# Four of the last sequence's eight attention steps placed ahead of the experts, in a kernel that runs two layers as one program

## The chip, the core and the metric

The kernel runs on one core of a Trainium2 chip. A core has TensorE (PE, matrix products, with PEld for its weight loads), VectorE (DVE), ScalarE (ACT), GpSimd (POOL) and SyncE (SP, which here only issues DMAs). Each engine works through its own list of instructions in order; semaphores hold an engine until another has got far enough. The metric is the device time of one execution in microseconds (us), as the median of several runs.

## The reference, cut to what matters

```python
x = L0_attn_x                                   # 8 sequences, 512 rows, 128 columns
xn = layernorm(x)
s = attention(xn, Wq, Wk, Wv, Wo)               # two query heads, one key/value head, rope, causal softmax
g = silu(experts(xn))                           # router, top 2 of 8 experts, F = 512, gelu
x = x + s * g
xn = layernorm(x)
s = mixer(xn)                                   # rmsnorm, 7-tap convolution, gated scan over the rows, gated ffn
g = silu(tanh(xn @ W @ A1 @ A2 + b))
x = x + s * g
```

Attention and experts of layer 0 read the same `xn` and don't need each other. The product `s * g` needs both.

## The kernel before

**The order of the stages.** There is no scheduler: each engine's list is written out by hand. (1) Layer norm, router and projections. (2) Attention of sequences 0 to 6 (`NB` = 7 is the number of the last one). Beside it POOL scatters the 2 x 4096 chosen rows to a DRAM buffer `slots_x`, sorted by expert, with 64 indirect DMAs in bursts of four. (3) The experts: 71 tiles of 128 rows (`SLOT_TILES`); PE does for each tile the gate product (L928), the up product (L937) and the down product (L946), one tile behind. (4) Attention of the last sequence. (5) Layer 1, sequence by sequence. Its first sequence has a long start: DVE adds the two expert rows of each token (`d_first_both`, L1463), multiplies with the attention (`d_first_product`, L1467), applies the gate (`d_first_gate`, L1472), adds to x (L1502), takes statistics (L1509), POOL takes the roots, DVE scales (L1480), and PE turns the result (`d_turn_scaled`, L983).

**One attention step.** A sequence has eight steps k, in the order of `STEPS = [(3, 0), (0, 0), (3, 1), (0, 1), (2, 0), (1, 0), (2, 1), (1, 1)]`: (tile of 128 rows, head). Tile i looks at i+1 tiles of keys, so the steps 0 to 3 and the steps 4 to 7 have the same sum of columns (1280 each). A step goes through four engines: scores on PE (L804, L806), row maximum on DVE (L1329), exponent on ACT (L1799), transposes on PE (L822), copy to SBUF on ACT (L1808), product with the values on PE (`weigh`, L844); for head 0 a scaled copy on ACT (`head0`, L1817), for head 1 a sum on DVE (`combine`, L1322). Three steps are under way at once: after scores k PE turns k-1 and weighs k-2. `finish` drains the last of them.

**What holds the experts back.** PE, DVE and ACT wait until the attention before the experts is through. ACT also waits for `w_ready` 3: POOL adds the third count after the scatter, with the last tap matrix of the convolution (L628). SP waits for all 64 scatters before it issues the loads of the first tiles (`XG`, L476), of the tags (L490, L493), and in the loop of the next experts' weights (L451).

**After the experts.** SP waits for the stores of the last two tiles, then loads the experts' rows of all sequences (L507). PE fills waits with products that nobody reads (`keep_warm`, L736).

Of the kernel before, what the change touches and what calls it, by code (L numbers as in the profile page):

```python
# [22 lines left out]
ALU = mybir.AluOpType  # L23
# [47 lines left out]
COMBINE_AFTER = {2: 0, 3: 1, 6: 2, 7: 3}  # L71

# [12 lines left out]
def build(nc, t, out):  # L85
    ctx = ExitStack()
    with ctx:
# [136 lines left out]
        def take():  # L224
# [119 lines left out]
            sem(n) for n in ("w_t1", "w_c1", "w_t2", "w_c2", "w_t3", "w_c3", "w_f1", "w_d1", "w_f2", "w_ready"))  # L344
        w_am = sem("w_am")
# [174 lines left out]
        def _(pool):  # L520
# [107 lines left out]
            pool.tensor_tensor(TAPW[:, PAD - KEPT, :], TAPW[:, PAD - KEPT, :], CHN[:, 0, :], ALU.add).then_inc(w_ready, 1)  # L628
# [101 lines left out]
        def _(pe):  # L730
# [125 lines left out]
            def attend(b, u, first=False, last=False):  # L856
                for k in range(NS):
# [3 lines left out]
                    if not last and k in PROJECT_AT[b == 0]:  # L861
                        project(b + 1, 1 - u, PROJECT_AT[b == 0].index(k))
                    if last and k == 1:
                        pe.wait_ge(c_yo, SLOT_TILES)
                        keep_warm(0, 5)
# [5 lines left out]
            def finish(b):  # L871
                turn(b, NS - 1)
                weigh(b, b % 2, NS - 2)
                weigh(b, b % 2, NS - 1)
# [44 lines left out]
            finish(NB - 1)  # L919
# [41 lines left out]
            pe.wait_ge(exp_done, NS * NB)  # L961
            pe.wait_ge(pt_done, NS * NB)
            pe.wait_ge(o_done, TPS * NB)
# [209 lines left out]
        def _(dve):  # L1173
# [162 lines left out]
            def attend(b, u, first=False, last=False):  # L1336
                for k in range(NS):
# [11 lines left out]
                    if last and k == 4:  # L1349
                        d_first_both()  # L1350
                    if last and k == 5:
                        d_first_product()
# [4 lines left out]
                    if k in ROPE_AT[b == 0] and not last:  # L1357
                        rope_begin(b + 1, ROPE_AT[b == 0].index(k))
                    if k - 1 in ROPE_AT[b == 0] and not last:
# [3 lines left out]
                    if last:  # L1363
                        if k == 6:
                            d_first_gate()
                        if k == 7:
                            d_stats(0)

            def finish(b):
                denominator(b, NS - 1)  # L1370
                combine(b, 2)
                combine(b, 3)
# [11 lines left out]
            finish(NB - 1)  # L1384
# [48 lines left out]
            dve.wait_ge(pv_done, NS * NB)  # L1433
            dve.wait_ge(o_done, TPS * NB)
# [257 lines left out]
            attend(NB, NB % 2, first=True, last=True)  # L1692
# [4 lines left out]
            finish(NB)  # L1697
# [27 lines left out]
        def _(act):  # L1725
# [93 lines left out]
            def attend(b, u, first=False, last=False):  # L1819
                for k in range(NS):  # L1820
# [18 lines left out]
                    if last:  # L1839
                        if k == 4:  # L1840
                            d_tanh(0)
                        if k == 6:
                            d_tanh(1)
                if not last:
                    values(b + 1, 1 - u)

            def finish(b):
                turned(b, NS - 1)
                head0(b, 3)
                bring_table(ACT.Gelu if b < NSEQ - 1 else ACT.Silu)  # L1850
# [15 lines left out]
            act.wait_ge(w_ready, 3)  # L1866
            finish(NB - 1)
# [27 lines left out]
            act.wait_ge(pv_done, NS * NB)  # L1895
            act.wait_ge(o_done, TPS * NB)
# [250 lines left out]
```

## Time and profile before

| what | value |
|---|---|
| runs, us | 538.95, 539.1, 540.4; median 539.1 |
| span of the profiled execution | 537.6 us (no time of its own is listed for it) |
| PE busy | 517.7 us, 96% of the span |
| DVE, ACT, POOL busy | 389.2, 314.6, 235.8 us |
| experts' first product on PE | 167.13 us |
| last sequence's first scores | 360.97 us |
| first transposes of layer 1 on PE | 378.79 us |

The span runs from the first to the last instruction that the profiler saw. The median lies 1.5 us above the profiled span. Busy time on PE includes waits inside its pipeline and the filler products, so 96% doesn't mean that PE is the limit everywhere: each stage is to be read by what its engines wait for.

### The profile page before, as it was taken

How to read it: one execution, taken by the hardware profiler on the slowest of the kernel's cores; microseconds unless marked ns; L12 is line 12 of the kernel's file. 1: busy time of each engine (PE TensorE's matmuls, PEld its weight loads, DVE VectorE, ACT ScalarE, POOL GpSimd, SP SyncE). 2: the span in 40 equal slices, each digit the busy share in tenths (PEclk: the TensorE clock that was granted, in tenths of full speed). 3: DMA queues.
4: the chain of work that ended last, by engine and by line, in shares of the span. 5: the costliest groups of instructions: out<-in, count | busy, mean ns of one | idle time of the engine just before them, and what ended most of it. 6: DMA issues, size and time to landing. Idle time of an engine off the chain costs nothing. (4 is left out here: it accounts for less than half of the span.)

```text
span 537.6 us, 12866 instructions
## 1 busy us (share of the span) xinstructions
PE 517.7 (96%) x3193; PEld 390.1 (73%) x3194; DVE 389.2 (72%) x1106; ACT 314.6 (59%) x830; POOL 235.8 (44%) x245
## 2 busy tenths in 40 slices
PE   9998999999976999999999999998999999999997
PEld 5756677767756999999999999986444545544544
DVE  6678877897762776777677767766688888788654
ACT  5535555555544666666666666667776576657511
POOL 4435765654560333333333333342667547624310
PEclk9999999999996999999999999999999999999999
DMA  8910123344317655555555555618300000000001
GB/s 248 392 72 15 37 98 107 107 119 154 128 45 53 153 146 150 143 152 143 151 141 156 138 157 134 160 38 231 87 1 20 1 20 22 20 0 21 20 8 33
DMA packets 85267, 54.00 MB, mean 100 GB/s; under 512 B 53088, under 2 KB 70016, under 8 KB 85104
## 3 DMA queue, kind: packets, MB, share of 16 engines
q1 hardware_dynamic: 80912, 44.66, 32.2%
q0 software_dynamic: 4320, 8.92, 4.6%
q8 instruction: 16, 0.26, 0.2%
q14 instruction: 19, 0.16, 0.1%
HBM read 37.82 MB, written 15.74 MB: 100 GB/s over the span
## 5 line engine op out<-in xcount | busy, mean ns | idle before, releaser
L1880 ACT ACTIVATE AR<-bank,BGT 128x128 f32<-128x128 f32 x284 | 81.3, 369 | 71.5 <-PE bank L928 71.5
L637 POOL DMA_INDIRECT rows_y<-YO,W1E x71 | 68.8, 969 | 119.6 <-DVE YO L1399 117.0
L1422 DVE SCALAR_TENSOR_TENSOR AR<-bank,B1T,AR 128x128 f32<-128x128 f32 x284 | 80.2, 344 | 7.7 <-PE bank L937 4.0
L594 POOL DMA_INDIRECT slots_x<-XR,SLOT x64 | 65.1, 1017 | 44.6 <-DMA slots_x<-XR,SLOT 28.9
L928 PE MATMUL bank<-AR,WGE 128*128 128x128 f32 x568 | 76.9, 279 | 1.6 <-DVE AR L1405 1.6
L937 PE MATMUL bank<-AR,WGE 128*128 128x128 f32 x568 | 76.0, 277 | 0.0
L946 PE MATMUL bank<-W2E,AR 128*128 x568 | 75.1, 275 | 0.5 <-DVE AR L1422 0.5
L928 PEld LDWEIGHTS bank<-AR,WGE 128*128 128x128 f32 x568 | 70.8, 196 | 1.9 <-issue 1.9
L937 PEld LDWEIGHTS bank<-AR,WGE 128*128 128x128 f32 x568 | 70.2, 195 | 0.0
L946 PEld LDWEIGHTS bank<-W2E,AR 128*128 128x128 f32 x568 | 69.1, 192 | 0.7 <-issue 0.7
L1799 ACT ACTIVATE AR<-bank,AR 128x512 f32<-128x512 f32 (+1 forms) x64 | 33.8, 528 | 54.4 <-DVE AR L1329 54.3
L844 PE MATMUL bank<-AR 128*128 128x128 f32 x320 | 48.3, 282 | 7.6 <-ACT AR L1817 6.7
L844 PEld LDWEIGHTS bank<-AR 128*128 128x128 f32 x320 | 41.2, 193 | 10.5 <-ACT AR L1808 9.8
L1329 DVE TENSOR_REDUCE AR<-bank 128x1 f32<-128x512 f32 (+1 forms) x64 | 31.1, 488 | 23.9 <-PE bank L806 23.5
L1405 DVE STREAM_TRANSPOSE AR<-XG 128x128 f32<-128x128 f32 x71 | 22.1, 312 | 35.8 <-PE bank L937 25.9
L1873 ACT ACTIVATE WGE<-SPARE 128x512 f32 x71 | 45.4, 641 | 1.8 <-DVE SA L1322 1.0
L804 PE MATMUL bank<-AR 128*128 128x128 f32 (+3 forms) x128 | 45.1, 436 | 0.0
L822 PEld LDWEIGHTS bank<-CST,AR 128*128 128x128 f32 x160 | 19.2, 140 | 23.1 <-ACT AR L1799 11.2
L2020 ACT ACTIVATE W1E<-bank 128x512 f32<-128x512 f32 x32 | 19.0, 593 | 26.9 <-PE bank L1070 26.9
L1808 ACT ACTIVATE AR<-bank 128x512 f32<-128x512 f32 (+1 forms) x64 | 27.5, 430 | 11.2 <-POOL TAPW L628 5.9
L1070 PE MATMUL bank<-WGE,WGT 128*128 128x512 f32 x64 | 32.7, 593 | 0.7 <-DVE X L1636 0.7
L1076 PE MATMUL bank<-WGE,WUP 128*128 128x512 f32 x64 | 32.7, 592 | 0.0
(216 smaller groups left out, 914.5 us busy)
## 6 DMA issues: line engine op xcount, KB each, us to landing
WGE<-in_wgu SPq DMA_DIRECT2D x71, 256.0 KB, 2.6
XG<-slots_x SPq DMA_DIRECT2D x140, 32.0 KB
slots_x<-W1E SPq DMA_DIRECT2D x7, 585.0 KB, 8.0
X<-in_x SPq DMA_DIRECT2D x8, 256.0 KB, 5.2
SPARE<-in_wgu SPq DMA_DIRECT2D x8, 256.0 KB
W2E<-in_w SPq DMA_DIRECT2D x8, 256.0 KB
XR<-rows_y SPq DMA_DIRECT2D x8, 256.0 KB, 5.0
XNT<-rows_y SPq DMA_DIRECT2D x8, 256.0 KB, 5.4
```

The lines of the kernel that those rows point to most:

```text
L594: pool.indirect_dma_start(out=slots_x, out_offset=bass.IndirectOffsetOnAxis(ap=SLOT[:, k, n:n + 1], axis=0), in_=XR[:, n, :], in_offset=No ...
L637: pool.indirect_dma_start(out=rows_y, out_offset=bass.IndirectOffsetOnAxis(ap=DST[:, j:j + 1], axis=0), in_=YO[q % 2][:], in_offset=None). ...
L804: pe.matmul(bank[:, 0:(i + 1) * P], QT[u][h][:, i * P:(i + 1) * P], QT[u][2][:, 0:(i + 1) * P], start=True, stop=False)
L844: mm = pe.matmul(reg, PT[k % 2][:, j * P:(j + 1) * P], U[u][:, j, h * P:(h + 1) * P], start=(j == 0), stop=(j == i))
L928: mm = pe.matmul(B[1 + u][:, c * P:(c + 1) * P], WB[:, q, c * P:(c + 1) * P], XT[u], start=True, stop=True)
L937: mm = pe.matmul(B[3 + u][:, c * P:(c + 1) * P], WU[:, u, c * P:(c + 1) * P], XT[u], start=True, stop=True)
L946: mm = pe.matmul(B[5 + u][:, 0:P], HT[u][:, c, :], W2E[:, bass.ds(e, 1), c, :], start=(c == 0), stop=(c == FC - 1))
L1070: pe.matmul(B[5 - 3 * (c % 2)][:], WGT[:, c * P:(c + 1) * P], H2, start=True, stop=True).then_inc(d_g, 1)
L1422: s = dve.scalar_tensor_tensor(out=HT[u][:, c, :], in0=B[3 + u][:, c * P:(c + 1) * P], scalar=B1T[:, bass.ds(e, 1), c], in1=ZB[u][:, c, :] ...
L1799: act.activation(PR[k % 2][:, 0:(i + 1) * P], B[2 + k % 2][:, 0:(i + 1) * P], ACT.Exp, bias=NM[:, k:k + 1], accum_out=DEN[:, k:k + 1]).the ...
L1873: act.activation(WU[:, u:u + 1, :], SPARE[:, bass.ds(e, 1), :], ACT.Copy).then_inc(c_wu, 1)
L1880: act.activation(ZB[u][:, c, :], B[1 + u][:, c * P:(c + 1) * P], ACT.Gelu, bias=BGT[:, bass.ds(e, 1), c]).then_inc(c_gelu, 1)
```

## The change

`AHEAD = 4`: steps 0 to 3 of the last sequence stand before the experts, right behind sequence 6, on PE, DVE and ACT (`attend_ahead`). They are drained there. Steps 4 to 7 stand behind the experts (`attend_rest`). The waits at the experts' start count four steps and two sums more. On DVE the start of layer 1 (`d_first_both` to `d_stats`), which stood between steps 4 and 7, follows the last sum. On ACT the two `d_tanh` follow the load of the Silu table. The last tap matrix has a semaphore of its own, `w_tap`, that only PE waits for, behind the experts; ACT no longer waits for it at the end of sequence 6. The filler ahead of the first transposes of layer 1 grows from 8 to 26 products. POOL and SP keep their lists.

```diff
+AHEAD = 4
+STEPS_AHEAD = NS * NB + AHEAD
+TILES_AHEAD = TPS * NB + AHEAD // 2
...
-            pool.tensor_tensor(TAPW[:, PAD - KEPT, :], ..., ALU.add).then_inc(w_ready, 1)
+            pool.tensor_tensor(TAPW[:, PAD - KEPT, :], ..., ALU.add).then_inc(w_tap, 1)
...
# PE
+            def attend_ahead(b, u):
+                for k in range(AHEAD):
+                    scores(b, u, k)
+                    turn(b if k >= 1 else b - 1, (k - 1) % NS)
+                    weigh(b if k >= 2 else b - 1, u if k >= 2 else 1 - u, (k - 2) % NS)
+                turn(b, AHEAD - 1)
+                weigh(b, u, AHEAD - 2)
+                weigh(b, u, AHEAD - 1)
+
+            def attend_rest(b, u):
+                for k in range(AHEAD, NS):
+                    scores(b, u, k)
+                    if k == AHEAD + 1:
+                        pe.wait_ge(c_yo, SLOT_TILES)
+                        keep_warm(0, 5)
+                    if k >= AHEAD + 1:
+                        turn(b, k - 1)
+                    if k >= AHEAD + 2:
+                        weigh(b, u, k - 2)
                 turn(b, NS - 1)
...
-            finish(NB - 1)
+            attend_ahead(NB, NB % 2)
...
-            pe.wait_ge(exp_done, NS * NB)
+            pe.wait_ge(exp_done, STEPS_AHEAD)
...
-            attend(NB, NB % 2, first=True, last=True)
-            finish(NB)
+            attend_rest(NB, NB % 2)
             pe.wait_ge(ld_up, 16 * N_UP)
-            pe.wait_ge(w_ready, 3)
+            pe.wait_ge(w_ready, 2)
+            pe.wait_ge(w_tap, 1)
...
-            keep_warm(3, 8)
+            keep_warm(3, 26)
...
# DVE
+            def attend_ahead(b):
+                for k in range(AHEAD):
+                    row_max(b, k)
+                    denominator(b if k else b - 1, (k - 1) % NS)
+                    if k in (1, 2):
+                        combine(b - 1, k + 1)
+                denominator(b, AHEAD - 1)
+                combine(b, 0)
+                combine(b, 1)
...
-            attend(NB, NB % 2, first=True, last=True)
+            attend_rest(NB)
+            d_first_both()
+            d_first_product()
+            d_first_gate()
+            d_stats(0)
             d_stats_settled(0)
...
-            finish(NB)
             d_first_scaled()
...
# ACT
+            def attend_ahead(b, u):
+                head0(b - 1, 3)
+                for k in range(AHEAD):
+                    if k == 3:
+                        head0(b, 0)
+                    exponent(b, k)
+                    turned(b if k else b - 1, (k - 1) % NS)
+                head0(b, 1)
+                turned(b, AHEAD - 1)
+                bring_table(ACT.Gelu)
...
-            act.wait_ge(w_ready, 3)
-            finish(NB - 1)
+            act.wait_ge(w_ready, 2)
+            attend_ahead(NB, NB % 2)
...
-            act.wait_ge(w_ready, 3)
-            attend(NB, NB % 2, first=True, last=True)
+            attend_rest(NB)
             finish(NB)
+            for b in range(2):
+                d_tanh(b)
             d_front2(2)
```

How the lists change. First PE at the end of sequence 6, before (AR holds the attention's and the experts' working tiles, CST the identity for transposes, WGE the gate weights; the last two rows are the first tile of the experts):

```order
L804 MATMUL bank<-AR 128x256
L806 MATMUL bank<-BFC 128x128
L792 MATMUL bank<-CVO,XNT 128x256 x4
L822 MATMUL bank<-CST,AR 128x128 x3
L844 MATMUL bank<-AR 128x128 x2
L822 MATMUL bank<-CST,AR 128x128 x2
L844 MATMUL bank<-AR 128x128 x5
L928 MATMUL bank<-AR,WGE 128x128 x4
L937 MATMUL bank<-AR,WGE 128x128 x4
```

And PE at the same place after the change: the last two of the four new steps' scores with what stands between them, the drain, and the first tile of the experts:

```order
L848 MATMUL bank<-AR 128x128 x2
L808 MATMUL bank<-AR 128x512
L810 MATMUL bank<-BFC 128x128
L826 MATMUL bank<-CST,AR 128x128
L848 MATMUL bank<-AR 128x128 x4
L808 MATMUL bank<-AR 128x128
L810 MATMUL bank<-BFC 128x128
L826 MATMUL bank<-CST,AR 128x128 x4
L848 MATMUL bank<-AR 128x128
L826 MATMUL bank<-CST,AR 128x128
L848 MATMUL bank<-AR 128x128 x5
L947 MATMUL bank<-AR,WGE 128x128 x4
```

The drain of sequence 6 (two and five products) is now spread between four new steps, whose own drain stands last; only then the first gate product.

DVE behind the experts, before, from the sixth maximum to the statistics of layer 1 (XR and XNT hold the experts' rows, W1E the tanh, SA the attention):

```order
L1329 TENSOR_REDUCE AR<-bank 128x1
L1334 RECIPROCAL AR<-AR 128x1
L1467 TENSOR_TENSOR SA<-XR,SA 128x512
L1322 SCALAR_TENSOR_TENSOR SA<-bank,AR 128x128
L1329 TENSOR_REDUCE AR<-bank 128x1
L1334 RECIPROCAL AR<-AR 128x1
L1322 SCALAR_TENSOR_TENSOR SA<-bank,AR 128x128
L1472 SCALAR_TENSOR_TENSOR XR<-W1E,SA 128x512
L1502 SCALAR_TENSOR_TENSOR X<-XR,X 128x512
L1329 TENSOR_REDUCE AR<-bank 128x1
L1334 RECIPROCAL AR<-AR 128x1
L1509 BN_STATS SPARE<-X 128x6 x4
```

And after the change, from the last reciprocal of the attention:

```order
L1353 RECIPROCAL AR<-AR 128x1 x2
L1341 SCALAR_TENSOR_TENSOR SA<-bank,AR 128x128 x2
L1487 TENSOR_TENSOR XR<-XR,XNT 128x512
L1491 TENSOR_TENSOR SA<-XR,SA 128x512
L1496 SCALAR_TENSOR_TENSOR XR<-W1E,SA 128x512
L1526 SCALAR_TENSOR_TENSOR X<-XR,X 128x512
L1533 BN_STATS SPARE<-X 128x6 x4
L1538 BN_AGGR SPARE<-SPARE 128x2 x4
L1544 SCALAR_TENSOR_TENSOR SPARE<-SPARE 128x4
L1547 SCALAR_TENSOR_TENSOR SPARE<-SPARE 128x4
L1482 SCALAR_TENSOR_TENSOR XR<-W1E,XR 128x512
```

The sums of layer 1's start stood between maxima, and now follow the whole attention. The gate of sequence 1 (L1458, now L1482) keeps its place behind the statistics.

## Rows read from the trace of the kernel before

**Rows 1.** The page: busy time and share per engine, granted clock in 40 slices.
```profile
PE 517.7 (96%) x3193; PEld 390.1 (73%) x3194; DVE 389.2 (72%) x1106; ACT 314.6 (59%) x830; POOL 235.8 (44%) x245
...
PEclk9999999999996999999999999999999999999999
```

**Rows 2.** Windows: busy per engine, PEclk, DMA share, GB/s, between attention and experts.
```profile
157.00:162.00 5.00, 0.61 (x6) 0.42 (x4) 0.35 (x1) 0.59 (x2) 3.66 (x4) 1.00 0.12 40
162.00:172.50 10.50, 6.56 (x29) 6.33 (x30) 2.32 (x8) 5.05 (x11) 0.64 (x2) 0.52 0.71 39
```

**Rows 3.** Timeline of PE, the experts' start: start, length, line, operation, [idle <-releaser].
```profile
156.37 0.38 PE L822 MATMUL bank<-CST,AR 128*128 128x128 f32 x2
...
164.29 1.19 PE L844 MATMUL bank<-AR 128*128 128x128 f32 x4 [6.68 <-ACT AR L1817]
167.13 2.04 PE L928 MATMUL bank<-AR,WGE 128*128 128x128 f32 x8 [1.65 <-DVE AR L1405]
...
174.31 1.06 PE L928 MATMUL bank<-AR,WGE 128*128 128x128 f32 x8
...
177.00 1.06 PE L928 MATMUL bank<-AR,WGE 128*128 128x128 f32 x8
```

**Rows 4.** Timelines of ACT, DVE and SP, in the same gap.
```profile
163.50 0.39 ACT L1808 ACTIVATE AR<-bank 128x256 f32<-128x256 f32 x1 [5.91 <-POOL TAPW L628]
...
164.16 1.28 ACT L1787 ACT_TABLE_LOAD   x1
...
165.52 0.35 DVE L1322 SCALAR_TENSOR_TENSOR SA<-bank,AR 128x128 f32<-128x128 f32 x1 [7.52 <-PE bank L844]
166.67 0.76 DVE L1405 STREAM_TRANSPOSE AR<-XG 128x128 f32<-128x128 f32 x2 [0.80 <-DMA XG<-slots_x]
...
162.91 2.06 SPq L476 DMA_DIRECT2D XG<-slots_x  x4
```

**Rows 5.** Timeline of PE: sequence 6, then the last sequence and what follows.
```profile
139.44 1.02 PE L804 MATMUL bank<-AR 128*128 128x512 f32 x2
...
151.02 0.39 PE L844 MATMUL bank<-AR 128*128 128x128 f32 x2
...
360.97 1.02 PE L804 MATMUL bank<-AR 128*128 128x512 f32 x2
...
370.39 0.39 PE L844 MATMUL bank<-AR 128*128 128x128 f32 x2
...
376.66 1.89 PE L736 MATMUL bank<-ONB 128*128 128x512 bf16 x8
378.79 0.63 PE L983 MATMUL bank<-CST,SPARE 128*128 128x128 f32 x4 [0.24 <-DVE SPARE L1480]
```

**Rows 6.** Timeline of DVE, the last sequence and the first steps of layer 1.
```profile
369.23 0.67 DVE L1463 TENSOR_TENSOR XR<-XR,XNT 128x512 f32<-128x512 f32 x1
...
372.31 0.68 DVE L1472 SCALAR_TENSOR_TENSOR XR<-W1E,SA 128x512 f32<-128x512 f32 x1
...
374.22 0.85 DVE L1509 BATCH_NORM_STATS2 SPARE<-X 128x6 f32<-128x128 f32 x4
...
377.42 1.12 DVE L1480 TENSOR_SCALAR SPARE<-X,SPARE 128x128 f32<-128x128 f32 x4 [0.21 <-POOL SPARE L664]
```

**Rows 7.** Timeline of POOL and DVE; line 1588 with durations min/median/max.
```profile
371.10 1.30 POOL L691 TENSOR_TENSOR XR<-XR,XNT 128x512 f32<-128x512 f32 x1 [7.25 <-DMA XNT<-rows_y]
...
399.02 1.71 POOL L677 TENSOR_TENSOR WGE<-WGE,SPARE 128x512 f32<-128x512 f32 x1 [2.88 <-DVE SPARE L1560]
...
400.12 1.16 DVE L1588 SCALAR_TENSOR_TENSOR SPARE<-W2E,VEC,SPARE 128x512 f32<-128x512 f32 x1
...
L1588 DVE SCALAR_TENSOR_TENSOR SPARE<-W2E,VEC,SPARE x35: 735/755/1575, 392.4 to 512.6; 128x512 f32<-128x512 f32 x35
```

**Rows 8.** DMA issues 160 to 190 us (count, size, us to landing), then SP's timeline.
```profile
WGE<-in_wgu SPq DMA_DIRECT2D x7, 256.0 KB, 4.2
...
W1E<-slots_x SPq DMA_DIRECT2D x1, 67.0 KB, 7.0
...
169.67 2.59 SPq L451 DMA_DIRECT2D WGE<-in_wgu  x1
172.31 1.90 SPq L476 DMA_DIRECT2D XG<-slots_x  x4
```

More of the change, by code:

```diff
@@ L627, in _ @@
             pool.wait_ge(w_am, TAPS - KEPT)
-            pool.tensor_tensor(TAPW[:, PAD - KEPT, :], TAPW[:, PAD - KEPT, :], CHN[:, 0, :], ALU.add).then_inc(w_ready, 1)
+            pool.tensor_tensor(TAPW[:, PAD - KEPT, :], TAPW[:, PAD - KEPT, :], CHN[:, 0, :], ALU.add).then_inc(w_tap, 1)
             def rows_of(first, end, part):
@@ L854, in count, with attend @@
                 pe.matmul(B[1][:, 0:NT * E], lowb, MB, start=True, stop=True).then_inc(r_cnt, 1)
-            def attend(b, u, first=False, last=False):
+            def attend(b, u, first=False):
                 for k in range(NS):
@@ L1334, in denominator, with attend @@
                 dve.reciprocal(RD[:, k:k + 1], DEN[:, k:k + 1]).then_inc(rd_done, 1)
-            def attend(b, u, first=False, last=False):
+            def attend(b, u, first=False):
                 for k in range(NS):
@@ L1356, in attend @@
                         combine(b - 1, k + 1)
-                    if k in ROPE_AT[b == 0] and not last:
+                    if k in ROPE_AT[b == 0]:
                         rope_begin(b + 1, ROPE_AT[b == 0].index(k))
-                    if k - 1 in ROPE_AT[b == 0] and not last:
+                    if k - 1 in ROPE_AT[b == 0]:
                         rope_end(b + 1, 1 - u, ROPE_AT[b == 0].index(k - 1))
@@ L1362, in attend, with attend_rest @@
                         experts((k - 1) // 2)
[L1363 to L1369, printed above, removed]
+            def attend_ahead(b):
[7 more added lines that the diff above has]
+                combine(b, 1)
+            def attend_rest(b):
+                for k in range(AHEAD, NS):
+                    row_max(b, k)
+                    if k > AHEAD:
+                        denominator(b, k - 1)
                 denominator(b, NS - 1)
@@ L1817, in head0, with attend @@
                 act.activation(O0[c], reg, ACT.Copy, scale=RD[:, k:k + 1]).then_inc(o0_done, 1)
-            def attend(b, u, first=False, last=False):
+            def attend(b, u, first=False):
                 for k in range(NS):
@@ L1838, in attend, with attend_rest @@
                                            scale=VEC[:, V_CONV + j:V_CONV + j + 1]).then_inc(w_am, 1)
[L1839 to L1845, printed above, removed]
+                values(b + 1, 1 - u)
+            def attend_ahead(b, u):
[8 more added lines that the diff above has]
+                bring_table(ACT.Gelu)
+            def attend_rest(b):
+                for k in range(AHEAD, NS):
+                    if k == NS - 1:
+                        head0(b, 2)
+                    exponent(b, k)
+                    if k > AHEAD:
+                        turned(b, k - 1)
             def finish(b):
@@ L1849, in finish @@
                 head0(b, 3)
-                bring_table(ACT.Gelu if b < NSEQ - 1 else ACT.Silu)
+                bring_table(ACT.Silu)
             def counted():
```

29 lines of the change are left out of this document (11 added, 18 removed).

## Prediction

> **What bounds the kernel now.** I read the page first: PE is busy for 96% of the span, at full clock in all slices but one [rows 1]. So the time can change where PE idles, where its clock is low, and where it works on something that nobody needs. The one slice with a lower clock lies between attention and experts. The windows around it [rows 2] show 0.61 us of PE work in the 5 us from 157, and then 10.5 us with a mean granted clock of 0.52, in which 6.56 us of work are done. The timeline of PE says what is waited for: a product of the last step of sequence 6 stands 6.68 us at 164.29 [rows 3], because ACT sits 5.91 us until POOL has added the last tap matrix, the third count of `w_ready` [rows 4]. POOL can add it only when the last scatters have landed, and SP's loads of the first tiles start then too (162.91). ACT then drains, loads the Gelu table (1.28 us), DVE makes the last sum (165.52 + 0.35 = 165.87), and its first expert transpose starts at 166.67, the arrival of the tiles being what is named [rows 4]. PE's first gate product follows at 167.13.
>
> Behind the experts the order is: the last sequence's scores at 360.97, its last products before 376.66, eight fillers, and at 378.79 the first transposes of layer 1 [rows 5]. Those wait for DVE's scaling (377.42), which waits for POOL's roots, which wait for the statistics (374.22) [rows 6]. So the tail is bound by DVE's chain and not by the attention's last products.
>
> **Front: what four steps cost there.** The change puts 1280 columns of scores, with their maxima, exponents, transposes and products with the values, into the gap. The nearest measure is the same four steps behind the experts: from 360.97 to 370.39 + 0.39 = 370.78, 9.8 us, drained in the shadow of later steps [rows 5]. I take 9.8 us for the new block, since the drain of sequence 6 lies in it (PE has that drain between the new scores, the fence on PE's list shows it). The block begins at 156.37, where PE stood ready to drain [rows 3]. It ends at 156.4 + 9.8 = 166.2. From the last sum to the first transpose took 166.67 - 165.87 = 0.8 us, from there to PE's gate 0.46 us [rows 3, 4]. First gate: 166.2 + 0.8 + 0.46 = 167.4, 0.3 us later than now. The tiles' loads aren't moved and had landed by 166.67. ACT isn't late: its last copy and the table fit before that sum, as they need only the scores' transposes; if the table ended 1 us later, ACT's weight copies would still be hidden behind the first gate product.
>
> **Front: what it brings.** PE no longer stands from 157.6 to 164.3, so I expect it at full clock when the experts begin. Now the five groups of eight products from the first gate (167.13) to the third (174.31) take 7.18 us. At full clock three groups take 177.00 - 174.31 = 2.69 us, so five take 4.48 us [rows 3]. Third gate: 167.4 + 4.5 = 171.9, 2.4 us sooner than 174.31. Bounds: with the block as slow as the same four steps in sequence 6, where projections and rope lie between (139.44 to 151.02 + 0.39, 12.0 us [rows 5]), the first gate is 2.2 us later and the gain 0.2. With a block so short that only the tiles' arrival counts, it is 2.7.
>
> **Is the gain kept?** The rest of the experts runs at 2.69 us per tile, bound by PE, so it must not meet a later supply. SP's list is unchanged, and the tags' load (67 KB in small pieces, 7.0 us to landing [rows 8]) starts when it did. Behind it the next weights' issue is stuck for 2.59 us at 169.67, and the tiles 4 and 5 are issued from 172.31 to 174.21. PE would now want tile 4 at 171.9 + 2 x 2.69 = 177.3 and not 179.7. Its weights, issued at 169.67 and 4.2 us on their way at the median, are there; the XG pieces had some 2.5 us after their last issue. This cover is thin, and if it is gone the price is up to the whole 2.4 us. POOL's stores of the first tiles wait for the same tags; a store is asked for only two tiles later.
>
> **The wait that goes.** `w_tap` takes ACT out of the wait for the scatter. Without the split the block would stand behind 163 again. Its price for PE is nothing: the count is there long before PE asks behind the experts.
>
> **Tail: attention.** Steps 4 to 7 have the same columns as 0 to 3. They begin at 360.97 and drain with nothing behind them, so I take 0.7 us off 9.8: last sum at 370.1. Then `d_first_both`, product, gate and addition, which now stand between maxima, come in a row: 0.67 and 0.68 us each [rows 6], with the handovers 3.0 us. Statistics at 373.1, not 374.22: 1.1 us sooner. The rows of the experts are there (DVE used them at 369.23 [rows 6]); ACT's tanh needs the Silu table, which is loaded while DVE makes the last sums. Of the chain behind the statistics nothing changes, so all of it shifts with them. The two sums that stood behind the gate of sequence 1 were hidden in the wait for POOL's roots.
>
> **Tail: what meets POOL.** POOL adds the rows of sequence 1 at 371.10, when they land, for 1.30 us [rows 7]. Now that falls between DVE's product (until about 371.5) and gate (due at 371.5). Before, DVE had sums and maxima from PSUM there. What a meeting costs can be read in layer 1: DVE's L1588 takes 0.755 us at the median, and 1.16 us at 400.12, where POOL's product ran from 399.02 to 400.73; it ends 0.55 us after POOL does. The longest L1588 is 1.575 us [rows 7]. So the gate waits out most of POOL's addition. Bounds: 0 (POOL comes when DVE is through) to 1.3 us (a whole addition). I take 0.9 us, near to the 0.8 between longest and median. The tail keeps 1.1 - 0.9 = 0.2 us.
>
> The Trainium skill, SBUF — State Buffer, section "SBUF: two separate sides", says that a VectorE operation with two SBUF inputs and a GpSimd operation that reads SBUF exclude one another for a whole instruction, the one that started first going through. By that rule gate and addition would be served after all of POOL's, and the tail's gain would be nothing; without it the tail would give the 1.1. The L1588 that ends 0.55 us behind POOL agrees with it.
>
> **Fillers.** The 26 fillers take, at 1.89 / 8 = 0.24 us each [rows 5], 6.1 us: from about 370.0 to 376.1, before the transposes, due at 378.6. They hold nothing up. PE idles 2.5 us behind them, where it idled 0.24.
>
> **Sum.** -2.4 at the front, -0.2 behind the experts: -2.6 us. The profiled span would go from 537.6 to 535.0; with the 1.5 us by which the median lies above the span, 536.5 us.
>
> **The rivals.**
> - *No meeting on DVE and POOL.* POOL's addition comes later or DVE's gate earlier. For it: a few tenths decide. Against: POOL is held by the product and is next. Then 539.1 - 2.4 - 1.1 = 535.6 us.
> - *The clock falls all the same*, in the 2.5 us gap behind the fillers. For it: it fell in the one long idle time. Against: that one began at 157.6, and the clock was still at full speed at 162, 4.4 us later [rows 2]. Price: like the spell at the experts' start, 7.18 - 4.48 = 2.7 us at most; I take 2.0, since a few of PE's products there wait for other engines anyway. Then 536.5 + 2.0 = 538.5 us.
> - *The supply holds the experts' start.* Tile 4 comes no earlier than now, behind the tags' load. For it: SP's stuck issue. Against: some 0.7 us of room by the sum above. The front gives nothing, the tail 0.2: 538.9 us.
> - *Slower: the two half blocks fill and drain like the interleaved ones.* Before, one block of eight steps was filled and drained once; now there are two. If each takes 12.0 us as in sequence 6, of the front's 2.4 us 12.0 - 9.8 = 2.2 are lost, and the tail's last sum is made at 373.3, the statistics at 373.3 + 3.0 + 0.9 = 377.2, 3.0 us later than now. Total 539.1 - 0.2 + 3.0 = 541.9 us. It decides from 1.3 us too much in each block on (2 x 1.3 = 2.6). Against: projections and rope don't stand in these blocks.
>
> **How the numbers follow.** My forecast has 0.50, no meeting 0.18, clock 0.13, supply 0.12, slow blocks 0.07. The forecast's own range is 535.8 to 537.3. The range of 8 in 10 goes from 535.0, 0.6 us below the case without meeting (front 2.7, and a tail shorter by a few tenths), to 538.9, the supply's; slow blocks and a little below lie outside. About 0.3% (1.6 us) is what a measurement can tell from no change: faster means under 537.5, slower above 540.7. Forecast and no meeting give faster nearly whole, with a twentieth of the others: 0.69. Clock and supply give same, with the forecast's edge: 0.24. Slower: 0.07.
>
> **What would show it.** Right: no slice with a lower clock between attention and experts; ACT's idle time behind sequence 6 gone, gate products 0.89 us apart from the first on; first gate near 167.4, last sequence's scores near 358.6; DVE's statistics 13.1 us behind those scores (now 374.22 - 360.97 = 13.25), and the gate L1496 at 1.1 us or more. Wrong: a first gate after 168.5; an idle PE before tile 4 or 5 that names a DMA; the block behind the experts longer than 10.4 us; a clock under 1.00 behind the fillers; a gate of 0.68 us, which is the case without meeting.

## The result, and the profile after

The changed kernel took 542.48 us at the median of six runs (541.74 to 545.17), the kernel before beside it 538.65 us (537.5 to 540.4). The ratio is 1.008, its 95% interval 1.0055 to 1.0104: slower by 0.8%. Forecast were 536.5 us and a chance of 0.07 for slower. The profiled run took 542.85 us, its span is 541.0 us (before: 537.6). Some executions of these kernels take some 8 us more, with everything from the first sequence on that much later and a granted clock of 0.61 to 0.64 between 20 and 34 us (1.00 in the others); medians and ratios leave out those more than 1.5% above the fastest of the same kernel, and of the profiles those of e7 and e12 show one, so that only stretches within them are compared.

I follow the path through both traces. First TensorE (PE) and VectorE (DVE) at the experts' start, in the kernel after.

```profile
156.59 1.02 PE L808 MATMUL bank<-AR 128*128 128x512 f32 x2
...
168.00 1.13 PE L947 MATMUL bank<-AR,WGE 128*128 128x128 f32 x8 [2.39 <-DVE AR L1429]
...
172.54 1.06 PE L947 MATMUL bank<-AR,WGE 128*128 128x128 f32 x8
...
178.48 1.15 PE L947 MATMUL bank<-AR,WGE 128*128 128x128 f32 x8 [0.42 <-DVE AR L1429]
...
165.42 0.61 DVE L1341 SCALAR_TENSOR_TENSOR SA<-bank,AR 128x128 f32<-128x128 f32 x2 [1.62 <-PE bank L848]
167.54 0.76 DVE L1429 STREAM_TRANSPOSE AR<-XG 128x128 f32<-128x128 f32 x2 [1.51 <-DMA XG<-slots_x]
...
178.03 0.31 DVE L1429 STREAM_TRANSPOSE AR<-XG 128x128 f32<-128x128 f32 x1 [1.75 <-DMA XG<-slots_x]
...
162.96 3.11 SPq L480 DMA_DIRECT2D XG<-slots_x  x4
...
169.63 3.92 SPq L455 DMA_DIRECT2D WGE<-in_wgu  x1
173.60 2.86 SPq L480 DMA_DIRECT2D XG<-slots_x  x4
...
163.07 0.45 POOL L632 TENSOR_TENSOR TAPW<-TAPW,CHN 128x128 f32<-128x128 f32 x1 [1.46 <-DMA slots_x<-XR,SLOT]
```

These rows answer to [rows 3, 4]. The block of four steps begins at 156.59 and its last two sums end at 166.03: 9.4 us. PE no longer stands 6.68 us for ACT. But the first gate (L947) comes at 168.00, since DVE's transposes wait 1.51 us for the tiles: SP's issue of the same four loads took 3.11 us, not 2.06. The third gate comes at 172.54, before at 174.31: 1.77 us sooner. SP then stands 3.92 us at 169.63 (2.59 before), and DVE waits 1.75 us for a tile at 178.03.

```profile
168.00:172.50 4.50, 4.50 (x40) 4.50 (x41) 2.19 (x9) 3.18 (x10) 0.19 (x1) 1.00 0.87 36
```

The window from the first to the third gate has a granted clock of 1.00 (the column behind the busy times and counts of PE, its weight loads, DVE, ACT and POOL); before, the window from 162 to 172.5 had 0.52 [rows 2].

Now one pass of the expert loop in DVE's timeline, the kernel before and then the kernel after. A pass is four tiles; L1405 and L1429 are the transposes, L1399 and L1423 the last products of a tile.

```profile
267.60 0.31 DVE L1405 STREAM_TRANSPOSE AR<-XG 128x128 f32<-128x128 f32 x1 [0.79 <-PE bank L937]
...
277.25 0.28 DVE L1399 TENSOR_SCALAR YO<-YB,W1E 128x128 f32<-128x128 f32 x1 [0.23 <-DVE YB L1390]
278.32 0.31 DVE L1405 STREAM_TRANSPOSE AR<-XG 128x128 f32<-128x128 f32 x1 [0.78 <-PE bank L937]
```

```profile
268.76 0.31 DVE L1429 STREAM_TRANSPOSE AR<-XG 128x128 f32<-128x128 f32 x1 [0.88 <-PE bank L956]
...
278.53 0.29 DVE L1423 TENSOR_SCALAR YO<-YB,W1E 128x128 f32<-128x128 f32 x1 [0.34 <-DVE YB L1414]
279.70 0.31 DVE L1429 STREAM_TRANSPOSE AR<-XG 128x128 f32<-128x128 f32 x1 [0.88 <-PE bank L956]
```

Before, a pass takes 278.32 - 267.60 = 10.72 us, after it 10.94. The loop's instructions are the same. The difference stands at two places: the last product waits 0.34 us and not 0.23 for its own predecessor, and the transpose at the head of a pass starts 0.88 us behind it, not 0.78. What it does to PE shows at the gate behind that transpose (PE's last down product of a pass and the next gate, before and then after):

```profile
277.94 1.06 PE L946 MATMUL bank<-W2E,AR 128*128 x8
278.83 1.06 PE L928 MATMUL bank<-AR,WGE 128*128 128x128 f32 x8
```

```profile
279.06 1.06 PE L965 MATMUL bank<-W2E,AR 128*128 x8
280.06 1.16 PE L947 MATMUL bank<-AR,WGE 128*128 128x128 f32 x8
```

Before, PE's groups of eight follow each other every 0.893 us all through the loop, and the twelve of a pass make the 10.72 us: PE did not wait. The gate began 0.20 us behind the end of DVE's transpose (278.63). After, it begins 1.00 us behind the group ahead of it and only 0.05 us behind the end of the transpose (280.01), and takes 0.1 us longer: now PE waits for DVE in each pass. The next gate comes at 282.85, 2.79 us later instead of 2.68. From the third gate to the last sequence's scores the kernel before took 360.97 - 174.31 = 186.66 us, the kernel after 363.54 - 172.54 = 191.00.

The tail, DVE and POOL and then PE, answers to [rows 5 to 7].

```profile
371.73 0.35 DVE L1341 SCALAR_TENSOR_TENSOR SA<-bank,AR 128x128 f32<-128x128 f32 x1 [0.28 <-PE bank L848]
...
373.52 0.69 DVE L1496 SCALAR_TENSOR_TENSOR XR<-W1E,SA 128x512 f32<-128x512 f32 x1
374.24 1.66 DVE L1526 SCALAR_TENSOR_TENSOR X<-XR,X 128x512 f32<-128x512 f32 x1
376.01 0.87 DVE L1533 BATCH_NORM_STATS2 SPARE<-X 128x6 f32<-128x128 f32 x4
...
379.23 1.11 DVE L1504 TENSOR_SCALAR SPARE<-X,SPARE 128x128 f32<-128x128 f32 x4 [0.94 <-POOL SPARE L668]
...
374.09 1.26 POOL L695 TENSOR_TENSOR XR<-XR,XNT 128x512 f32<-128x512 f32 x1 [7.67 <-DMA XNT<-rows_y]
...
371.53 5.78 PE L740 MATMUL bank<-ONB 128*128 128x512 bf16 x26
380.60 0.63 PE L1002 MATMUL bank<-CST,SPARE 128*128 128x128 f32 x4 [3.30 <-DVE SPARE L1504]
...
391.91 1.02 PE L1056 MATMUL bank<-WGE,WST 128*128 128x512 f32 x2
```

The last sum ends 372.08 - 363.54 = 8.5 us behind the scores (forecast 9.1). POOL's addition (374.09) meets DVE's own addition: 1.66 us. The statistics come 12.47 us behind the scores (before 13.25, forecast 13.1), the first transposes of layer 1 17.06 us (before 17.82). PE waits 3.30 us there. The windows behind it:

```profile
380.60:382.00 1.40, 1.27 (x7) 0.65 (x7) 0.50 (x1) 0.67 (x1) 0.87 (x1) 0.95 0.98 289
382.00:384.00 2.00, 1.93 (x3) 0.90 (x4) 1.74 (x12) 0.89 (x3) 1.26 (x1) 0.50 0.62 183
384.00:386.00 2.00, 2.00 (x5) 0.91 (x4) 0.54 (x2) 1.66 (x3) 1.64 (x1) 0.68 0.00 1
```

The clock fell to half, by the means of these windows for some 3.4 us (an estimate). From the transposes to the product L1056 (L1037 before) the kernel after needs 391.91 - 380.60 = 11.31 us; before, 388.53 - 378.79 = 9.74. From there to the end both take 149.1 us.

So the span's +3.4 us are: third gate -1.77; from there to the last sequence's scores +4.34; tail -0.76; half clock +1.57.

### The profile page after: what moved, and what is told of

Same layout as the page of the kernel before. It is cut to its first block and busy times, and to the rows that moved or that the text cites. A ratio compares the mean times of both kernels' runs of the same rounds, so it can differ in the third digit from the quotient of the medians.

```text
span 541.0 us, 12903 instructions
## 1 busy us (share of the span) xinstructions
PE 524.0 (97%) x3211; PEld 390.7 (72%) x3212; DVE 390.5 (72%) x1106; ACT 315.2 (58%) x830; POOL 235.1 (43%) x245
## 5 line engine op out<-in xcount | busy, mean ns | idle before, releaser
L947 PE MATMUL bank<-AR,WGE 128*128 128x128 f32 x568 | 76.8, 278 | 3.0 <-DVE AR L1429 3.0
L947 PEld LDWEIGHTS bank<-AR,WGE 128*128 128x128 f32 x568 | 69.0, 192 | 5.7 <-issue 3.3
L956 PEld LDWEIGHTS bank<-AR,WGE 128*128 128x128 f32 x568 | 69.1, 192 | 0.0
L1429 DVE STREAM_TRANSPOSE AR<-XG 128x128 f32<-128x128 f32 x71 | 22.1, 312 | 39.4 <-PE bank L956 34.9
L1423 DVE TENSOR_SCALAR YO<-YB,W1E 128x128 f32<-128x128 f32 x71 | 20.3, 286 | 18.0 <-DVE YB L1414 17.0
```

Source lines behind the costliest of these rows:

```text
L947: mm = pe.matmul(B[1 + u][:, c * P:(c + 1) * P], WB[:, q, c * P:(c + 1) * P], XT[u], start=True, stop=True)
L956: mm = pe.matmul(B[3 + u][:, c * P:(c + 1) * P], WU[:, u, c * P:(c + 1) * P], XT[u], start=True, stop=True)
```

## The experiments

Fourteen runs were made, in four groups: e1 to e4 on chip 7, e5 to e8 on chip 3, e9 to e11 and e12 to e14 on chip 6. Each group had runs of the kernel before beside it. The table reads the same stretches in every trace. "Tap matrix" is POOL's addition that ends the scatter's work; "turn" stands for the first transposes of layer 1; state is the product L1037/L1056.

```
                    tap    1st gate 3rd gate  3rd gate  scores   turn to  pass   time   ratio to before
                    matrix                    to scores to turn  state           us     (95% interval)
before              163.02 167.13   174.31    186.66    17.82     9.74    10.72  538.65
after               163.07 168.00   172.54    191.00    17.06    11.31    10.93  542.48 1.008 (1.0055-1.0104)
e1  40 fillers      159.57 167.73   173.76    190.08    17.04     9.74    10.94  541.52 1.0041 (0.9998-1.0085)
e2  before +12      163.36 167.47   173.97    190.09    18.13     9.74    10.94  543.39 1.0093 (1.0033-1.0154)
e3  after +28       160.76 167.33   171.87    188.30    17.04    10.92    10.82  539.12 1.001 (0.9963-1.0056)
e4  w_tap alone     158.66 162.77   170.00    186.61    17.83     9.74    10.72  537.79 0.997 (0.9918-1.0022)
e5  after +52, 40f  160.58 168.80   173.34    188.10    17.15     9.74    10.82  540.73 1.0077 (1.004-1.0114)
e6  e5 + 4 fillers  160.40 169.88   174.42    188.08    17.14     9.74    10.82  540.28 1.0042 (1.002-1.0065)
e7  e4 + fillers    169.93 175.43   179.89    187.13    17.92     9.73    10.72  538.42 0.9999 (0.998-1.0017)
e8  before +6       162.13 166.39   172.94    186.59    19.68     9.71    10.72  539.88 one run
e9  after +26, 40f  162.18 171.37   175.91    188.28    17.19     9.73    10.82  541.34 1.0076 (1.0041-1.0111)
e10 e9 + 4 fillers  162.83 172.08   176.62    188.31    17.04     9.74    10.82  540.93 1.0061 (1.0036-1.0086)
e11 two steps ahead 160.98 166.03   170.49    186.73    19.06     9.74    10.72  536.91 0.9977 (0.9946-1.0009)
e12 before again    170.18 174.28   180.55    186.63    17.82     9.73    10.72  545.61 one run
e13 after again     161.15 169.35   175.52    190.08    17.04     9.74    10.93  543.43 1.0105 (1.0084-1.0126)
e14 after +28, 40f  163.79 169.75   174.29    188.30    17.04     9.74    10.82  542.65 1.0078 (1.0059-1.0096)
```

The medians of the kernel before were 539.33 us beside e1 to e4, 537.68 beside e5 to e8, 537.67 beside e9 to e11 and 538.49 beside e12 to e14. e1 to e4 rest on four executions each, so their intervals are wide.

**More fillers (e1).**

```
-            keep_warm(3, 26)
+            keep_warm(3, 40)
```

> The changed kernel with 40 instead of 26 fillers behind the last attention products. Theory (clock): the 26 fillers end at 377.3, PE idles 3.3 us, and the clock falls to half at about 381.9; 14 more fillers at 0.22 us end at about 380.3, just before the first transposes of layer 1 are due at 380.6. Then the granted clock stays at 1.00 from 380 to 386, the way from those transposes to the state product (11.3 us in the changed kernel) takes 9.7 us as in the kernel before, and the time is 1.6 us less: about 540.9 us. Rival (the spell at half clock is hidden behind DVE's chain of layer 1, whose scan also ends later there for another reason): the clock stays up, but that way takes over 11 us and the time moves by less than 0.4 us. If the fillers run past 380.6 they delay the transposes: that would show as no idle time ahead of them.

The 1.57 us came back (turn to state 9.74). This run also showed something else, at the experts' start:

```profile
167.73 2.05 PE L947 MATMUL bank<-AR,WGE 128*128 128x128 f32 x8 [1.69 <-DVE AR L1429]
...
168.00:170.00 2.00, 2.00 (x10) 2.00 (x10) 0.04 (x1) 0.48 (x2) 0.00 (x0) 0.50 1.00 11
```

The scatter had ended 3.5 us earlier, so the block itself set the first gate, and behind it PE stood 1.69 us. Its clock was at half all through 168 to 170. The third gate came 14.2 us behind the tap matrix, where the kernel before needs 10.4 to 11.3 (its own traces, e2, e4, e8 and e12).

**The loop's place (e2, e3).** A row of waits that are long fulfilled goes ahead of the loop in DVE's list; two waits make one instruction, N instructions in all. Nothing else changes.

```
+            for _ in range(2 * N):
+                dve.wait_ge(r_texp, 1)
             finish(NB - 1)          # e2: kernel before, N = 12;  e3: attend_ahead(NB), N = 28
```

> The kernel before, with 12 instructions more on DVE ahead of the experts, each a wait for something long done, in the time in which DVE idles there. They move DVE's loop over the expert tiles from its instruction 474 to 486, where the changed kernel has it. Nothing else changes. In the changed kernel DVE takes 10.93 us for the four tiles of one pass of the loop, against 10.72 before, with 0.1 us more ahead of the last product of a pass and 0.1 us more behind the branch. Theory A (place of the loop's code): the pass takes 10.93 us here too, over 16 passes 3.4 us more, some of it covered by slack at first: 541.5 to 542.2 us. Theory B (phase: the first tiles' late supply leaves DVE and PE in another rhythm): the pass stays at 10.72 us and the time at 538.7 us.

> The changed kernel, with 28 instructions more on DVE ahead of the experts, each a wait for something long done, ahead of the four new steps. They move the loop from instruction 486 to 514. A loop of 95 instructions that begins at 474 crosses one multiple of 64 (512), one that begins at 486 crosses two (512 and 576), one that begins at 514 again one (576). Theory A (place of the code, with such a step): the pass takes 10.72 us again and the time is about 3 us less, 539.5 us; the front may lose up to 0.5 us of it by the waits themselves. Theory B (phase): 10.93 us per pass and 542.5 us. If the pass takes yet another value, the place matters but the step is another one.

The change had moved the loop from instruction 474 to 486 of DVE's list. The kernel before, moved by the same 12, shows the same two waits:

```profile
269.26 0.31 DVE L1407 STREAM_TRANSPOSE AR<-XG 128x128 f32<-128x128 f32 x1 [0.88 <-PE bank L937]
...
279.04 0.29 DVE L1401 TENSOR_SCALAR YO<-YB,W1E 128x128 f32<-128x128 f32 x1 [0.34 <-DVE YB L1392]
280.20 0.31 DVE L1407 STREAM_TRANSPOSE AR<-XG 128x128 f32<-128x128 f32 x1 [0.88 <-PE bank L937]
```

It takes 190.09 us from third gate to scores, as e1 and e13 do: 3.4 us over the 186.66 before, with no step moved. The kernel after at 514 has a pass of 10.82 us and 188.30. So this loss hangs on where the loop stands, and nothing else of the change. e2's tail is also 0.3 us longer. The median of e2 is 4.1 us above that of the kernel before, 543.39 against 539.33, which is 1.0075; the ratio of 1.0093 has one execution of 548.12 us in it.

**The semaphore alone (e4).** The kernel before, with POOL's addition counted on `w_tap` and ACT waiting for `w_ready` 2.

> The kernel before with the split of the semaphore alone: ACT no longer waits for the last tap matrix at the end of sequence 6, no step is moved. Theory: attention drains at 158 instead of 165.5, PE then idles until the experts' first tiles have landed at 166.6, a gap of some 8 us, so the clock is still low at the experts' start: the first gate product comes at 167.1 at the earliest and takes 2.0 us as before; time within 0.6 us of 538.7. Rival (the wait itself cost the start): the first gate product comes over 1 us sooner and the time falls by 1 us or more. If the clock is up at the start although PE idled, the gain of the moved steps was not in the clock.

From the tap matrix to the first gate e4 took 4.11 us, the kernel before 4.11: ACT's wait of 5.91 us [rows 4] had cost nothing, because the tiles' loads come at the same moment. And this scatter ended 4.4 us sooner than in the first profile, and with it the first gate: 162.77. With four steps ahead it can't come before some 166.9, by the block's earliest first scores (156.17, e3) and the 10.7 us from there to the gate in e1 and e13 (an estimate).

**Both repairs, and fillers ahead of the first gate (e5, e6, e9, e10).** As e1 and e3 together. In e5 and e6 104 waits stand ahead of sequence 0, which put the loop at 538; in e9 and e10 52 waits ahead of the block, loop at 512; e6 and e10 have also `keep_warm(5, 4)` in front of the first gate.

> The change with 40 fillers instead of 26, and with 104 waits on VectorE for the router's logits (long there) put ahead of its first maximum, where it waits 3.71 us anyway; two of them fold into one instruction, so the expert loop starts at instruction 538 of VectorE's code in place of 486: at 474, where the kernel before has it, plus 64. Theory (the loop costs by its place, and places repeat every 64 instructions): a pass takes 10.72 us again, the last sequence's scores come 0.21 x 14 = 2.9 us sooner than in the run with 40 fillers alone, about 360.9, turn to state product 9.74 us, and the time is 541.5 - 2.9 = 538.6; where the scatter ends early or the supply holds, up to 1.8 us less. Rival 1 (only fewer boundaries count, not the place modulo 64): pass 10.82, time 540.0. Rival 2 (the added block itself slows the loop, by its buffers or transfers): pass 10.93, time 541.5.

> As the run before it in this call, with 4 more fillers (0.9 us) on TensorE between the block that stands ahead and the first gate. In the run with 40 fillers alone TensorE idled 1.69 us there and its clock was 0.86 and then 0.50 behind it: the first gate took 2.05 us instead of 1.13. Theory: the fillers leave under 0.9 us of idling where the block is the bound and about 1.5 us where the scatter is, so the clock stays at 1.00 more often; mean time 0 to 0.7 us below the run before it, never above by more than 0.1 (the first gate waits for VectorE's transposes for longer than the fillers take). Rival: the clock was lost for another reason than the gap, no difference.

> The change with 40 fillers and 52 waits (26 instructions) ahead of the block, which put VectorE's expert loop at instruction 512: it ends at 606, just below 608, and starts at a multiple of 32, as the loop at 480 did (10.72 us a pass). Theory (loop place and clock are the whole of the loss behind the front): pass 10.72 us, turn to state product 9.74 us; against the run with 28 instructions more (539.1: pass 10.82, 10.92 us from turn to state) 1.4 and 1.2 us less = 536.5. Where the scatter ends early the block is the bound, so against the kernel before the gain shrinks to the tail's 0.8 us: 537.5. Rival (the place acts by more than these two): pass 10.82, time 538.

> The run before it in this call with 4 fillers (0.9 us) more between the block and the first gate. In the earlier pair of this kind the clock was 1.00 at the first gate in both profiles, and the median was 0.2 us apart. Theory: it helps only in the executions in which the clock falls in that gap (first gate 2.05 us instead of 1.13, some 1.3 us in all), so 0 to 0.7 us less than the run before it; rival: nothing or 0.2 us more.

Wrong in both terms. The pass was 10.82 us in all four, so places don't repeat every 64 instructions, and my rule for 512 was wrong too. And the times stayed 0.4 to 0.8% above the kernel before, though the clock and half of the loop's loss were repaired (third gate to scores 188.1 to 188.3, between 186.66 and 190.09). What was lost besides lies ahead of the experts: the third gate comes 12.8 to 14.0 us behind the tap matrix. DVE stands still inside the sequences. The same piece of sequence 2, in the kernel before and in e9 (DVE's timeline):

```profile
74.33 0.29 DVE L1329 TENSOR_REDUCE AR<-bank 128x1 f32<-128x128 f32 x1 [0.41 <-PE bank L806]
```

```profile
76.36 0.29 DVE L1348 TENSOR_REDUCE AR<-bank 128x1 f32<-128x128 f32 x1 [2.07 <-remote]
```

"Remote" names no engine of the core. Such stops add up: e9's first maximum of the block comes at 161.78, that of e3 at 157.38. From the attention's first scores to the second 512-column scores of sequence 6 the kernels take 110.1 to 110.2 us in the first two profiles and in e1 to e4, which show no such stop, and 111.5 to 113.3 us in e5 to e14, which all do. In e5 and e6 the run's time also lies 2.1 to 2.5 us above its span, elsewhere 1.8 to 1.9; I can't say why. The four fillers brought 0.4 us at the median in both pairs, with intervals that overlap, so no gain is shown; the clock was up at the first gate in all four profiles, so they had nothing to repair there.

**The clock without moved steps (e7).** The kernel of e4, and on PE, ahead of the first tile:

```
+            keep_warm(5, 18)
+            pe.wait_ge(w_tap, 1)
+            keep_warm(5, 10)
```

> The kernel before with its own semaphore for the tap matrix and nothing moved; TensorE gets 18 fillers (4 us) ahead of the experts, then waits for the tap matrix (POOL's work behind the scatter), then 10 more (2.2 us). Theory (at the front the change only kept TensorE's clock up, the moved steps did nothing else): clock 1.00 at the first gate, which comes 4.1 us behind the tap matrix or later by up to 2 us where the scatter ends early; third gate 4.6 us behind the first instead of 7.2; pass 10.72 us, scores 17.8 us ahead of the turn, as before. Time: 537.8 (semaphore alone) less 1 to 2.4 = 535.4 to 536.8, under both kernels. Rival 1: the supply of weights and inputs gives the gain back within the first nine tiles, as in the profile of the change (1.77 us sooner at the third gate, 0.38 at the ninth): 537.4. Rival 2: the clock is not up without real steps between the fillers: 537.8.

The third gate came 9.96 us behind the tap matrix (before 11.29, and 10.37 to 11.34 in its other traces), the clock was 1.00. The time did not follow: ratio 0.9999. Of the 0.4 to 1.4 us gained at the third gate, 0.5 us were lost again before the scores; what became of the rest is open.

**Six instructions (e8).**

> The kernel before with VectorE's expert loop 6 instructions further on (at 480 instead of 474), by 12 waits ahead of its first maximum. It ends at 574, just below 576, a multiple of 64. Theory (a multiple of 64 near the loop's end costs 0.11 us a pass, and 0.10 us behind the branch goes by the distance from the loop's start to the next multiple): the end costs nothing, behind the branch 0 or 0.10 us, so a pass of 10.72 or 10.82 us. Rival (any move from 474 costs the same): 10.93.

At 480 the pass is 10.72 us, which is PE's own time, so a still shorter loop of DVE wouldn't show. But the tail took 19.68 us and not 17.82: here DVE's gate and its scaling met POOL.

```profile
370.88 1.25 DVE L1474 SCALAR_TENSOR_TENSOR XR<-W1E,SA 128x512 f32<-128x512 f32 x1
...
376.69 2.15 DVE L1482 TENSOR_SCALAR SPARE<-X,SPARE 128x128 f32<-128x128 f32 x4
```

1.25 and 2.15 us, in the first profile 0.68 and 1.12 [rows 6]. A shift of tenths decides which operation meets POOL.

**Two steps ahead (e11).** `AHEAD = 2`; the first steps of layer 1 interleaved with the remaining six as before the change; 8 fillers there, at the front `w_tap` and 10 fillers ahead of the first tile.

> The change with two steps ahead instead of four, and what follows from it: the last layer's first steps stand among the remaining six steps again, as before the change, 8 fillers there, and at the front 10 fillers behind a wait for the tap matrix. VectorE's loop starts at 478 and ends at 572. Theory: the block ends by 162, so the first gate is bound by the scatter again (4.1 us behind the tap matrix) with the clock up: third gate 9.0 to 10 us behind the tap matrix (before 11.3, the change 9.5); pass 10.72 us; at the tail two steps fewer take 3.4 us off, of which the data for the last layer's first sum may hold back up to 3 (before, that sum came 8.3 us behind the last scores without waiting). Time: 538.5 - 1.3 to 2 (front) - 0.4 to 3.4 (tail) = 533 to 537. Rival 1 (the tail is bound by the expert outputs' rows, not by the steps): 537. Rival 2 (a meeting of VectorE and POOL in the tail costs 1 to 1.9 us, as in the loop at 480): 538.

```profile
163.87 2.32 PE L740 MATMUL bank<-ONB 128*128 128x512 bf16 x10
166.03 1.05 PE L947 MATMUL bank<-AR,WGE 128*128 128x128 f32 x8
...
364.53 0.69 DVE L1500 TENSOR_TENSOR XR<-XR,XNT 128x512 f32<-128x512 f32 x1 [2.38 <-DMA XNT<-rows_y]
...
367.90 1.64 DVE L1539 SCALAR_TENSOR_TENSOR X<-XR,X 128x512 f32<-128x512 f32 x1
...
373.89 2.13 DVE L1517 TENSOR_SCALAR SPARE<-X,SPARE 128x128 f32<-128x128 f32 x4
```

The third gate comes 9.51 us behind the tap matrix. In the tail rival 1 and rival 2 both hold: DVE waits for the experts' rows until 364.53, and meets POOL twice (1.64, 2.13). 536.91 us, beside 537.67: the best median of all, but the interval reaches to 1.0009, so it isn't shown to beat the kernel before.

**The kernels themselves again (e12 to e14).** e12 and e13 are unedited; e14 is e1 and e3 together.

> The kernel before, unedited, with a profile from the same chip as the two kernels next to it. In the seven runs of the last two calls VectorE stood still for 1 to 2 us at several places of sequences 1 to 6, which the first calls did not show, and sequence 6's last steps came 2 to 5 us later. Theory (the chip, not the edits, does this): here too, the maxima of 512 come later by over 1 us against the first profile, unless this chip is one without such stops; the scatter's end stays where it is (158.5 to 163.5), since POOL waits for none of it, and the first gate comes 4.1 us behind the tap matrix all the same: the stops cost the kernel before nothing. Rival (the edits brought the stops): none here, maxima at 140.5 and 144.4.

> The changed kernel, unedited, on the same chip. Theory: its block starts where sequence 6 ends, so stops in the sequences move the first gate, which comes 10.7 us behind the block's first scores or 4.1 to 5 us behind the tap matrix, whichever is later. With stops it loses 2 to 4 us at the first gate against a chip without: ratio 1.010 to 1.014; without stops 1.004 to 1.009 as at first. The loop's pass is 10.93 us, turn to state product 11.3 us either way.

> The change with 40 fillers and with the 28 instructions ahead of the block (pass 10.82 us in the first call). Theory: against the changed kernel next to it 1.5 us less from the loop and 1.2 to 1.6 us less from TensorE's clock = 2.7 to 3.1 us less; against the kernel before 537.6 to 538 against 538.5 on a chip without stops (same or slightly faster), 1.003 to 1.008 on one with. Rival (the repaired losses come back elsewhere): under 1.5 us less than the changed kernel.

The stops are in the unedited kernels too. The maximum that was shown above for e9, in e12:

```profile
83.67 0.29 DVE L1329 TENSOR_REDUCE AR<-bank 128x1 f32<-128x128 f32 x1 [1.43 <-PE bank L806]
```

It names PE, but PE's scores had ended at 82.62; in the first profile the maximum starts 0.03 us behind them, here 1.05. Counted from its own first maximum, e12's sequence 6 lies 3.2 us later than in the first profile. So the edits didn't bring the stops. They cost the kernel before nothing that shows: its medians beside e5 to e14 are 537.67 to 538.49, beside e1 to e4 539.33. What they cost is read at the first gate. The kernel before (PE's products of sequence 6 and first gate, POOL's tap matrix):

```profile
171.45 1.19 PE L844 MATMUL bank<-AR 128*128 128x128 f32 x4 [2.52 <-ACT AR L1817]
174.28 2.04 PE L928 MATMUL bank<-AR,WGE 128*128 128x128 f32 x8 [1.64 <-DVE AR L1405]
...
180.55 1.06 PE L928 MATMUL bank<-AR,WGE 128*128 128x128 f32 x8
...
170.18 0.45 POOL L628 TENSOR_TENSOR TAPW<-TAPW,CHN 128x128 f32<-128x128 f32 x1 [1.45 <-DMA slots_x<-XR,SLOT]
```

and the kernel after:

```profile
158.66 1.02 PE L808 MATMUL bank<-AR 128*128 128x512 f32 x2
...
169.35 1.76 PE L947 MATMUL bank<-AR,WGE 128*128 128x128 f32 x8 [1.68 <-DVE AR L1429]
...
175.52 1.06 PE L947 MATMUL bank<-AR,WGE 128*128 128x128 f32 x8
...
167.48 0.61 DVE L1341 SCALAR_TENSOR_TENSOR SA<-bank,AR 128x128 f32<-128x128 f32 x2 [1.62 <-PE bank L848]
168.90 0.77 DVE L1429 STREAM_TRANSPOSE AR<-XG 128x128 f32<-128x128 f32 x2 [0.80 <-DVE SA L1341]
...
161.15 0.45 POOL L632 TENSOR_TENSOR TAPW<-TAPW,CHN 128x128 f32<-128x128 f32 x1 [1.45 <-DMA slots_x<-XR,SLOT]
...
170.00:172.00 2.00, 2.00 (x12) 2.00 (x11) 0.00 (x0) 0.76 (x4) 0.00 (x0) 0.50 0.74 15
```

Before, the first gate follows the tap matrix by 4.10 us here and by 4.11 to 4.26 us in its other traces, e2, e4 and e8, whatever happened in the sequences. After, it follows the block's first scores by 10.69 us (168.90 names DVE's own sum, not a tile), here 8.2 us behind the tap matrix; and behind a gap of 1.68 us PE ran at half clock. Third gate 14.4 us behind the tap matrix, before 10.4. The ratio of e13 is 1.0105. By the two ratios e14 takes 0.27% or 1.5 us less than e13 (by the medians 0.8 us; the intervals overlap), where I expected 2.7 to 3.1: in e13's profile the clock had not fallen behind the 26 fillers (turn to state 9.74, after the same 3.28 us of idling that cost 1.57 in the first profile and 1.18 in e3), so only the loop's 1.8 us are sure to come back.

## Why the prediction was wrong, step by step

The forecast was -2.6 us, the span grew by 3.4. The 6.0 us between them are the loop's 3.43, the wait at tile 4 with 0.91, the clock in the tail with 1.57 and 0.63 missing at the third gate, less 0.56 by which the tail did better.

- *Block of 9.8 us, under cover.* Length right (9.4). But "156.4 + 9.8 = 166.2" set it against the scatter of one execution, where it would make the first gate only 0.3 us later. The tap matrix comes at 158.66 to 163.79 in the traces without the 8 us shift, and the block never ends before 165.7 (e3). With an early scatter or with stops in the sequences the block is the bound. e1, e4 and e13 show this.
- *First gate 167.4, third gate 2.4 us sooner.* 168.00 and 1.77: 0.6 us off, by SP's slower issue. The clock was at full speed, as forecast; not in e1 and e13, where the block was the bound and PE idled 1.7 us behind it.
- *"Is the gain kept?" "The rest of the experts runs at 2.69 us per tile, bound by PE".* The step that failed. In the kernel before PE was the bound, as said, with 10.72 us a pass. But DVE's loop had next to no slack, and its length hangs on its place in the list: moved from 474 to 486, it made the pass 10.94 us, with PE waiting. Cost 3.4 us in every trace at 486 (after, e1, e2, e13), more than the whole forecast gain. The sum put this at nothing: it had no term for instructions that stand ahead of a loop. The thin cover of tile 4 did give way in the first profile: 0.9 us (191.00 - 190.08), in no other run of the change.
- *The wait that goes costs nothing.* Right, but it also brings nothing to the first gate (e4).
- *Tail: 1.1 us sooner, less 0.9 for meeting POOL.* 0.78 sooner at the statistics (0.2 forecast) with a meeting of 1.66 - 0.69 = 0.97 in it. The addition met POOL in place of the gate, which took 0.69: my sign for "no meeting" came, and there was one. The size of the meeting was right. That agrees with what the Trainium skill says in SBUF — State Buffer, section "SBUF: two separate sides", of VectorE and GpSimd excluding one another; DVE's addition ends 0.55 us behind POOL's, as L1588 did [rows 7]. What made the tail better than forecast is that steps 4 to 7 took 8.5 us and not 9.1.
- *Clock behind the fillers*, a rival with 0.13, happened: 1.57 us, against 2.0 priced. The argument against it (4.4 us without a fall after 157.6) didn't hold: it fell behind 3.3 us here and behind 3.28 in e3, though not in e13.
- *Slower* had 0.07 and another mechanism (slow half blocks), which did not occur. The supply rival came in part (0.9 us, in one execution).

## What to carry to other kernels

Before moving work into a gap, ask what ended the gap in other executions: if the end wanders (here 5 us with the scatter), only a block that fits the shortest gap is free. Where two engines keep pace in a loop, treat both as the bound, and compare a pass of the loop before and after, even if its instructions are the same. Give fillers for the whole of a new idle time: with 40 the clock held in all six profiles, with 26 it fell in two of three.

## What the hardware did that I had not expected

- A pass through a loop of 95 DVE instructions takes 10.72 us from 474, 478 and 480 (PE's own time, so DVE may need less there), 10.93 to 10.94 from 486, 10.82 from 512, 514 and 538. Why the place counts no run shows, and the rule for the places is open.
- DVE stood still for 0.5 to 2.1 us at places of straight code in every trace of chips 3 and 6 (e5 to e14) and in none of chip 7 (e1 to e4). Whether it goes with the chip or with the moment is not shown.
- The clock fell to half behind idle times of 1.68 (e13), 1.69 (e1), 3.28 (e3) and 3.30 us (after), and stayed up behind 3.28 (e13), 2.04 (e3) and 1.68 (e5): the length alone does not decide.
